# A six-layer transformer stack on one core: who scales, who halves and who adds the residual in the one-layer mixture

## The reference

```python
x = x + 0.5 * _L0_ffn_ref(_layernorm(x), ...)     # MOE0_A: 16 experts, two matmuls each, gelu, top 2
x = x + _L0_attn_ref(_layernorm(x), ...)          # ATT0: linear attention over 256 tokens
x = x + 0.5 * _L0_ffn_ref(_layernorm(x), ...)     # MOE0_B
x = x + 0.5 * _L1_ffn_ref(_layernorm(x), ...)     # MOE1_A: 16 experts, one layer each
x = x + _L1_attn_ref(_layernorm(x), ...)          # ATT1: causal linear attention, 16 heads
x = x + 0.5 * _L1_ffn_ref(_layernorm(x), ...)     # MOE1_B
```

```python
logits = jnp.einsum('bsh,eh->bse', tokens, gate_w)
weights = jax.nn.softmax(logits, axis=-1)
top2_w, top2_idx = jax.lax.top_k(weights, 2)
y = jax.nn.relu(jnp.einsum('nh,edh->ned', flat, expert_w) + expert_b[None, :, :])
sel = jnp.take_along_axis(y, flat_idx[:, :, None], axis=1)
out = jnp.sum(sel * flat_w[:, :, None], axis=1)
```

## Time and profile before

| | us |
|---|---|
| median of 3 runs | 738.96 |
| lowest, highest | 737.16, 744.51 |
| the profiled execution | 736.88 |
| its span, from first to last instruction | 735.2 |
| granted TensorE clock over the span | 0.955 of full |

### The profile page before, as it was taken

One profiled execution on the slowest core, in us unless ns is written; L12 is line 12 of the kernel. 1 busy time (PEld: TensorE's weight loads), 2 busy tenths in 40 slices (PEclk: granted clock), 3 DMA queues, 4 the chain that ended last, 5 costly groups with the idle time before them and its releaser, 6 DMA issues.

```text
span 735.2 us, 7595 instructions
## 1 busy us (share of the span) xinstructions
PE 656.1 (89%) x2395; PEld 417.7 (57%) x2395; DVE 509.0 (69%) x1139; ACT 403.9 (55%) x795; POOL 214.4 (29%) x148
## 2 busy tenths in 40 slices
PE   3699998999999999999999998999999869868693
PEld 2456565555555565665666665566666445555472
DVE  5587457647446636658599687869776468688887
ACT  4254464546545544766754695584476325745394
POOL 2120010110002202181320364041037136775367
PEclk9899998999999999999999999999999969989897
DMA  8772522053243134512223232103221000000001
GB/s 244 153 152 63 111 58 58 20 97 58 60 105 66 59 68 79 73 26 46 58 58 70 48 58 58 57 3 91 72 41 27 1 0 0 1 0 16 14 1 29
DMA packets 27027, 42.23 MB, mean 57 GB/s; under 512 B 1689, under 2 KB 8938, under 8 KB 26986
## 3 DMA queue, kind: packets, MB, share of 16 engines
q1 hardware_dynamic: 26986, 41.74, 26.5%
HBM read 40.42 MB, written 1.31 MB: 57 GB/s over the span
## 4 chain that ended last, share of the span: by engine, by line
PE 38%; DVE 25%; issue 19%; POOL 11%; ACT 6%; DMA 0%; SPq 0%; DVEq 0%; POOLq 0%; ACTq 0%
PE py L1103 14%; PE ph L882 4%; PE ph L883 4%; PE ph L884 4%; POOL stage L440 3%; POOL rstd L387 3%; POOL stage L444 3%; DVE xn L659 2%; DVE red L769 2%; DVE hw L841 2%; ACT stage L528 2%; DVE stage L766 1%; DVE stage L736 1%; DVE X L771 1%; PE ps L1057 1%
## 5 line engine op out<-in xcount | busy, mean ns | idle before, releaser
L577 ACT ACTIVATE g<-ph,b1col 128x512 f32<-128x512 f32 x256 | 171.9, 689 | 146.6 <-PE ph L884 111.8
L1103 PE MATMUL py<-hw,w2s 128*128 128x512 f32 x512 | 249.0, 611 | 2.4 <-DVE hw L841 2.4
L841 DVE TENSOR_TENSOR hw<-g,bc 128x1024 f32<-128x1024 f32 x128 | 166.1, 1301 | 94.7 <-ACT g L577 93.2
L387 POOL TENSOR_TENSOR rstd<-vare,mhalf 128x4 f32<-128x4 f32 x24 | 36.6, 1524 | 392.2 <-DVE vare L653 392.2
L1103 PEld LDWEIGHTS py<-hw,w2s 128*128 128x128 f32 x512 | 97.6, 194 | 78.5 <-issue 64.9
L882 PE MATMUL ph<-xbh,w1h 128*128 128x512 f32 x256 | 135.1, 528 | 0.0
L528 ACT ACTIVATE stage<-ps,comb 128x128 f32<-128x128 f32 x288 | 84.1, 514 | 44.4 <-PE ps L1013 28.5
L883 PE MATMUL ph<-xbl,w1h 128*128 128x512 f32 x256 | 103.4, 404 | 0.0
L884 PE MATMUL ph<-xbh,w1l 128*128 128x512 f32 x256 | 103.3, 404 | 0.0
L882 PEld LDWEIGHTS ph<-xbh,w1h 128*128 128x128 f32 x256 | 49.9, 195 | 28.5 <-issue 20.6
L883 PEld LDWEIGHTS ph<-xbl,w1h 128*128 128x128 f32 x256 | 50.1, 196 | 24.0 <-issue 17.0
(11 more groups left out here) (207 smaller groups left out, 959.7 us busy)
## 6 DMA issues: line engine op xcount, KB each, us to landing
bc<-comb_rows SPq DMA_DIRECT2D x31, 1024.0 KB, 8.5
stage<-in_L_ffn_W_dram SPq DMA_DIRECT2D x4, 512.0 KB, 6.9
X<-in_L_attn_x_dram SPq DMA_DIRECT2D x4, 256.0 KB, 3.3
bc<-comb_rows SPq DMA_DIRECT2D x4, 256.0 KB, 5.6
out_dram<-X SPq DMA_DIRECT2D x4, 256.0 KB, 2.3
comb_rows<-combT SPq DMA_DIRECT2D x8, 32.0 KB, 2.1
side<-in_L_attn_wq_dram SPq DMA_DIRECT2D x1, 64.0 KB
side<-in_L_attn_wk_dram SPq DMA_DIRECT2D x1, 64.0 KB
```

Source lines behind the costliest of these rows:

```text
L387: nc.gpsimd.tensor_tensor(rstd[:, 0:n], vare[:, 0:n], mhalf[:, 0:n], ALU.pow).then_inc(light["rstd"], 1)
L577: nc.scalar.activation(g[:, s % 2, h, 0:w], ph[:, (HC * s + h) % RING_PH, 0:w], ACT.Gelu, bias=b1col[:, HC * e + h:HC * e + h + 1]).then_i ...
L841: V.tensor_tensor(hw[:, s % RING_HW, :, 0:w], g[:, s % 2, :, 0:w], bc[:, s // GQ % 2, s % GQ, 0:w].unsqueeze(1).to_broadcast([P, HC, w]), ...
L1103: ins = T.matmul(py[:, 0:cols], w2s[:, w], hw[:, s2 % RING_HW, h, 0:cols], start=e2 == 0 and h == 0, stop=False)
```

## The change

1. ACT_GROUPS becomes (4, 4): in both lanes ACT takes all four groups of a tile, and DVE none.
2. POOL adds the second half of the tile's buffer to the first with one instruction of 1024 columns, in place of L438, L440 and L444. The branch for fewer ACT groups is there but not taken, and all four entries of QUARTERED are False.
3. DVE sums eight experts with one reduction of 1024 columns into one of two buffers (red and red_late are doubled) and signals "sum". L766 and L771 are gone.
4. POOL adds the sum to X and signals "red". It does so one tile late: after the next tile's addition, and for the last tile of a piece as a step of its own. The factor 0.5 is put into the routing weights (for MOE1) in the instruction that makes comb.
5. lgs, oh1, selm, topf, s_all and s_rec move from SBUF to the second half of the pl bank. `light_bank` now waits on "comb" when the stage before was rt.
6. The light list begins with chunk 1 before chunk 2, and c0 of MOE0_B's chunk 0 comes before the normalization for ATT0's chunk 1.
7. All four strings of TURNS are new.

```diff
-    ACT_GROUPS = 3
+    ACT_GROUPS = (4, 4)
...
+    QUARTERED = {(MOE1_A, 0): False, (MOE1_B, 0): False, (MOE1_A, 1): False, (MOE1_B, 1): False}
...
-        red = sb("red", [P, D])
-        red_late = sb("red_late", [P, D])
+        red = sb("red", [P, 2, D])
+        red_late = sb("red_late", [P, 2, D])
...
+        small = pl[:, CH // 2:CH]
+        lgs, oh1, selm = (small[:, i * TPC * E:(i + 1) * TPC * E].rearrange("p (t e) -> p t e", t=TPC) for i in range(3))
+        topf = small[:, 3 * TPC * E:3 * TPC * E + 2 * TPC].rearrange("p (t a) -> p t a", t=TPC)
+        s_all, s_rec = (small[:, 3 * TPC * E + i * TPC:3 * TPC * E + (i + 1) * TPC] for i in (2, 3))
...
+                def residual(j):
+                    pool.wait_ge(signal["sum"], n + j + 1)
+                    nc.gpsimd.tensor_tensor(X[:, tile_(c, j)], X[:, tile_(c, j)], total[:, (n + j) % 2, :], ALU.add).then_inc(signal["red"], 1)
+
                 for j in range(ntiles(c)):
-                    pool.wait_ge(signal["relu_a"], (n + j + 1) * ACT_GROUPS)
...
+                    if acts == GROUPS:
+                        pool.wait_ge(signal["relu_a"], (n + j + 1) * acts)
+                        both, other = (r[:, j % 2, a * E * D // 2:(a + 1) * E * D // 2] for a in range(2))
+                        nc.gpsimd.tensor_tensor(both, both, other, ALU.add).then_inc(signal["half"], 2)
...
+                    yield
+                    if j:
+                        residual(j - 1)
+                        yield
+                residual(ntiles(c) - 1)
+                yield
...
-                                act.wait_ge(signal["red"], n + j - 1)
+                                act.wait_ge(signal["sum"], n + j - 1)
...
-                V.tensor_tensor(comb[:, tiles(c), :], t_(pm), r_(s_rec).unsqueeze(2).to_broadcast([P, n, E]), ALU.mult).then_inc(light["comb"], 1)
+                V.scalar_tensor_tensor(comb[:, tiles(c), :], t_(pm), 1.0 if moe0(l) else 0.5, r_(s_rec).unsqueeze(2).to_broadcast([P, n, E]),
+                                       ALU.mult, ALU.mult).then_inc(light["comb"], 1)
...
-                    xs_ = X[:, tile_(c, j)]
-                    ins = V.scalar_tensor_tensor(xs_, sum_[:, :], 0.5, xs_, ALU.mult, ALU.add)
-                    ins.then_inc(signal["red"], 1)
+                        V.tensor_reduce(sums, r[:, j % 2, 0:E * D // 2].rearrange("p (a d e) -> p d a e", a=2, d=D), mybir.AxisListType.XY, ALU.add).then_inc(signal["sum"], 1)
...
-                    signal = {"ln": "xl", "rt": "shift", "ct": "ct"}[last]
+                    signal = {"ln": "xl", "rt": "comb", "ct": "ct"}[last]
```

More of the change, by code:

```diff
@@ L203, in build_program @@
                                           "vz", "o_ps", "o", "x")}
-        f1 = {(l, late): {n: sem(f"f{l}_{late}_{n}") for n in ("y_ps", "relu_a", "relu_v", "half", "quarter", "red")}
+        f1 = {(l, late): {n: sem(f"f{l}_{late}_{n}") for n in ("y_ps", "relu_a", "relu_v", "half", "quarter", "sum", "red")}
               for l in (MOE1_A, MOE1_B) for late in (0, 1)}
@@ L434, in f1_ @@
                 r = rel_late if late else rel
+                acts = ACT_GROUPS[late]
+                total = red_late if late else red
+                def residual(j):
+                    pool.wait_ge(signal["sum"], n + j + 1)
+                    nc.gpsimd.tensor_tensor(X[:, tile_(c, j)], X[:, tile_(c, j)], total[:, (n + j) % 2, :], ALU.add).then_inc(signal["red"], 1)
                 for j in range(ntiles(c)):
-                    pool.wait_ge(signal["relu_a"], (n + j + 1) * ACT_GROUPS)
@@ L442, in f1_ @@
-                    if l == MOE1_A:
+                    if acts == GROUPS:
+                        pool.wait_ge(signal["relu_a"], (n + j + 1) * acts)
+                        both, other = (r[:, j % 2, a * E * D // 2:(a + 1) * E * D // 2] for a in range(2))
+                        nc.gpsimd.tensor_tensor(both, both, other, ALU.add).then_inc(signal["half"], 2)
+                    else:
+                        pool.wait_ge(signal["relu_a"], (n + j + 1) * acts)
+                        nc.gpsimd.tensor_tensor(r0, r0, r2, ALU.add).then_inc(signal["half"], 1)
+                        pool.wait_ge(signal["relu_v"], (n + j + 1) * (GROUPS - acts))
+                        nc.gpsimd.tensor_tensor(r1.rearrange("p (d e) -> p d e", d=D), r1.rearrange("p (d e) -> p d e", d=D),
+                                                r3.rearrange("p (e d) -> p d e", d=D), ALU.add).then_inc(signal["half"], 1)
@@ L443, in f1_ @@
+                    if QUARTERED[l, late]:
                         pool.wait_ge(signal["half"], 2 * (n + j + 1))
-                        nc.gpsimd.tensor_tensor(r0, r0, r2, ALU.add).then_inc(signal["quarter"], 1)
+                        nc.gpsimd.tensor_tensor(r0, r0, r1, ALU.add).then_inc(signal["quarter"], 1)
                     yield
+                    if j:
[3 more added lines that the diff above has]
+                yield
@@ L747, in f1_ @@
                 late, signal, n = moe1(l, c)
-                banks, r, sum_ = (ph, rel_late, red_late) if late else (ps, rel, red)
+                banks, r, total = (ph, rel_late, red_late) if late else (ps, rel, red)
+                acts = ACT_GROUPS[late]
                 for j in range(ntiles(c)):
                     for q in range(GROUPS):
-                        if q >= ACT_GROUPS:
+                        if q >= acts:
                             if j == 0:
@@ L760, in f1_ @@
                         yield
-                    if l == MOE1_A:
+                    if n + j >= 2:
+                        dve.wait_ge(signal["red"], n + j - 1)
+                    sums = total[:, (n + j) % 2, :]
+                    if QUARTERED[l, late]:
                         dve.wait_ge(signal["quarter"], n + j + 1)
+                        V.tensor_reduce(sums, r[:, j % 2, 0:E * D // 4].rearrange("p (d e) -> p d e", d=D), AX, ALU.add).then_inc(signal["sum"], 1)
                     else:
                         dve.wait_ge(signal["half"], 2 * (n + j + 1))
-                        r0, r2 = (r[:, j % 2, a * E * D // 4:(a + 1) * E * D // 4] for a in (0, 2))
-                        (klink if late else hlink)(V.tensor_tensor(r0, r0, r2, ALU.add))
-                    if j:
-                        dve.wait_ge(signal["red"], n + j)
-                    (klink if late else hlink)(V.tensor_reduce(sum_[:, :], r[:, j % 2, 0:E * D // 4].rearrange("p (d e) -> p d e", d=D), AX, ALU.add))
-                    xs_ = X[:, tile_(c, j)]
-                    ins = V.scalar_tensor_tensor(xs_, sum_[:, :], 0.5, xs_, ALU.mult, ALU.add)
-                    ins.then_inc(signal["red"], 1)
+                        V.tensor_reduce(sums, r[:, j % 2, 0:E * D // 2].rearrange("p (a d e) -> p d a e", a=2, d=D), mybir.AxisListType.XY, ALU.add).then_inc(signal["sum"], 1)
                     yield
```

25 lines of the change are left out of this document (10 added, 15 removed), and 35 rows, old and new, of the table TURNS.

## The result

The changed kernel takes 703.9 us (median of 4 runs, 700.03 to 708.19), the kernel before beside it 741.5 (4 runs, 737.16 to 744.51): a ratio of 0.950 with a 95% interval of 0.942 to 0.958. The forecast was 723 and its range 713 to 735, so the sign was right and the gain was twice as large as forecast: 37.6 us by the medians.

A forecast was written before the change was run, and what follows sets the result against it. The prediction took PE to bound the main loop to 586 us and a chain of waits the tail: 735.2 less 18.6 plus 3 made a span of 719.6, plus 1.7 and 2.1 for the median 723 us, range 713 to 735.

The forecast's parts named there:

- the main part's price: Main loop, up to 586 us: ACT's 12.4 us of new relus hidden and the routings' later weights free, taken as 0.
- The tail: The 149.2 us after the main loop, walked in stages to 130.6, which is 18.6 less, before 3 for the clock.
- A: Tail, from the main loop's end to the routing weights of MOE1_A: 20.9 us instead of 19.9.
- B: Tail, from MOE1_A's routing weights to the start of the statistics for attention: 25.2 us instead of 36.9.
- C: Tail, from the statistics for attention to the late attention's qkv matmuls: 10.7 us instead of 8.6.
- D: Tail, from the qkv matmuls to the late attention's last addition: 36 us instead of 40.7.
- the 3 us for the clock: Tail: some 12 of 80 groups paced by PE at half clock, 0.25 us each, adding 3 us.
- E: Tail, from the late attention's last addition to MOE1_B's routing weights: 14 us instead of 13.9.
- F: Tail, from MOE1_B's routing weights to the last residual: 21.0 us instead of 26.4.
- ACT takes DVE's place: Rival, in the tail: the 20.6 us of new relus all lie on the chain, giving 740 us; chance 0.17.
- The main loop stalls: Rival: PE waits behind relu bursts and for routing weights, up to 28 us, giving 751 us; chance 0.08.
- The port: Rival: POOL's longer additions hold up DVE's normalizations on the chain by 2 to 5 us, giving 725 to 728; chance 0.15.

The follow-up runs named there:

- Exchanging code and turns: Against the kernel before: changed code with all old turns 0.997; with only the main loop's new turns 0.973; with only the tail's new turns 0.977.
- the second profile: Profile of a repeat of the changed kernel, nothing edited; 705.25 us, 0.949 to the kernel before.
- small_in_sbuf: Changed kernel with lgs, oh1, selm, topf, s_all and s_rec back in SBUF; 709.8 us, 0.956 to the kernel before.
- residual_on_dve: Changed kernel with the residual back on DVE, right behind its reduction; 710.1 us, 0.956 to the kernel before.
- the shift of 17 entries: Kernel before, with 17 entries of PE's turns changed so that transposes of a normalized chunk stand half a slot later; 731.95 us, 0.986.

## Why the prediction was right and wrong

**The step that failed** is the main part's price. It was put together from two halves, a cost with bounds 0 to 28 and, as the other end, "a gain ... which PE's waits bound at 16.2", and the value taken was 0. The loop gained 14.2 by its end (idle time 40.3 to 25.5), and 17 like for like by the two profiles, with the 2.9 us of chunk 2's qkv that moved into it. The bound was taken from the right row, PE's 11 waits for the normalization, but it was no bound: 5.5 of its 16.2 are the start-up's and stayed, so 10.7 was all that this wait could give. PE's idle time fell by 14.8, of which 11.1 are this wait and the rest PE's waits for other steps. What was wrong is its mechanism: the prediction tied it to DVE waiting less for POOL, a relief by the code. Exchanging code and turns shows that the code took 5.0 us off these waits and at most 0.7% off the time, and that the order gives nearly everything. The working gave every edit of the code a price and read the new turns only for what they could harm ("the turns leave heavy groups or a slot between"). It never laid the new places of PE's transposes beside the 11 waits, though both are in the diff and the trace. The range then stopped at 713, although 16.2 of possible gain was in hand, and 723 less 14 is 709. With the loop right, the forecast would have been near 709 against 703.9 and 705.3 measured. The rest is the choice of executions: the forecast added 2.1 for the median's distance from the profiled execution of before; the changed kernel's median lies 4.3 below its own.

**The tail** was right in sum, 133.6 against 134.4, with errors that cancel and with luck in the execution: the second profile has 130.0. A is 3 us shorter than put, since chunk 2's qkv was done ahead of the loop's end (it lies in the 571.8). B was put at 25.2 and took 28.2: the late relus, an early group and a copy were walked in 19 and took 21.3 (589.70 to 611.04), with one wait of 2.35 for PE at their head that the walk did not have; from there it was 6.8 for the 6.1 put, and POOL does the early addition at 614.30 ahead of the late residual at 616.66, as said. The order that had sent POOL to an early tile first did go. C: 10.7 put, 10.1 measured. D was put at 36 and took 39.6 and 37.1: PE is busy 38.35 of the 39.6 at a clock of 0.91, so it seems to be PE that fills this stage now (read from the windows; no run took work off PE). The prediction walked ACT and POOL through D and not PE; the 3 us for the clock, one sum over all stages, belonged mostly here. E 14 and 14.5, F 21 and 21.3, with ACT filling F as said.

**Durations.** Put and measured: POOL's addition 2.5 and 2.39; its residual 0.5 and 0.46; DVE's reduction 1.22 and 1.22; ACT's group 1.03 and 1.06 (16.92 for 16); DVE's total 472 and 465.5; POOL's 181 and 181.3. Nearest rows of the same operation carried all of these. The routing buffers in PSUM cost nothing to be seen, as by the row: 3 to 8 ns an instruction by the lines above. The rule of the Trainium skill ("VectorE: DVE Perf Modes", the TRN2 errata) would have it at 65 ns, an estimate from its figures; the trace doesn't agree.

**The rivals.** ACT takes DVE's place: half true in its mechanism. ACT is what C, E and F wait for in part, but at a price below DVE's. The main loop stalls: no; ACT's wait for PE stayed (120.1 us of idle time ahead of the gelus, 111.8 before), and no burst held a gelu long enough to reach PE. The port: real, and smaller than its room. DVE in the tail of the changed kernel (start, us):

```profile
619.17 1.68 DVE L672 TENSOR_SCALAR vare<-mv 128x4 f32<-128x4 f32 x1
620.86 1.22 DVE L790 TENSOR_REDUCE red<-stage 128x128 f32<-128x1024 f32 x1
622.26 3.46 DVE L678 TENSOR_SCALAR xn<-X,mv,rstd 128x128 f32<-128x128 f32 x4 [0.18 <-POOL rstd L388]
625.64 1.21 DVE L790 TENSOR_REDUCE red<-stage 128x128 f32<-128x1024 f32 x1
```

POOL runs an addition from 618.43 to 620.83 and one from 622.57 to 624.97. The four normalizations take 3.46, where they took 1.10 with POOL idle (578.40), and a four-column addition takes 1.68; the reductions beside them keep 1.22. That is 2.4 and 1.5 us more in C. The rule named with the rival, in the Trainium skill's "SBUF — State Buffer" (Who interferes with whom), agrees with both halves of this. C still came out at 10.1, because ACT's relus (34 of them up to the copy) are as long: on the chain the port's hold is hidden beside them. The same hold is what small_in_sbuf and residual_on_dve bring back, each 0.7% slower: taking small two-operand instructions and the residual off SBUF and DVE was likely part of the gain, and the prediction's sum has neither as a gain.

**What stays open.** Of the main turns' 2.4%, the shift of 17 entries accounts for about 1.4; which of the other moves bring the rest, and whether the new code was needed to make them, was not taken apart. Nor was the new tail's order run under the old mixture code. Part of the difference by medians (9 of 37.6 us) goes with the granted clock of single executions: the changed kernel's four runs have 0.964, 0.967, 0.972 and 0.977 at 708.2, 704.8, 703.0 and 700.0 us. Why the executions are granted different clocks no run here tells.

## What to carry to other kernels

Where the order of each engine's work is written out by hand, a diff of that order is as large an edit as a diff of the code: lay the new places of every waiting instruction beside the waits that the trace names, and put the whole of those waits into the range as a possible gain. Relieving an engine (35 us off DVE here) gives next to nothing while the order still makes the others meet it at the same places; order without relief gave 1.4%, both together 5%. And when work is given back to an engine, look at what now stands in front of its other steps: DVE's scaling, put a tile ahead, waited for PE and held the reduction that ACT's buffer waits for, and the tile took 4.5 us where ACT's part had come down to 3.3.

## What of the hardware was not expected

- An ACTIVATE of 512 columns that writes its outputs apart from each other (the experts interleaved) took 0.99 us in a row, hardly less than four of 128 columns, 1.03. One such instruction alone lasts 1.17 us; a gelu of 512 columns from PSUM to contiguous columns (L596) lasts 0.69. On DVE the group's scaling took 1.07 with such a write and 0.68 with a contiguous one.
- A POOL power of four columns takes 1.01 us at the least (median 1.48) and an addition of 128 columns 0.46, of 512 columns 1.29, of 1024 columns 2.39.
- A DVE instruction of 64 columns with two SBUF operands took 2.45 us beside POOL's addition of 1024 and 0.22 otherwise; with one operand in PSUM it took 0.23 at the most.
- The whole time follows the granted clock closely: 0.977 against 0.964 is 1.3%, and 700.0 against 708.2 us is 1.2%, in runs of one kernel one after another.
